# Attention products in column tiles of 32, and new orders at both ends of the shared feed-forward

## The chip, the cores and the metric

The kernel runs on one core of a Trainium2 chip. The metric is the device time of one execution in microseconds. TensorE is PE in the rows (its weight loads are PEld), VectorE is DVE, ScalarE is ACT, GpSimd is POOL, and SyncE is SP, which here only issues DMAs.

## The reference

Four sequences of 1024 tokens, 256 features. One layer: attention, then a mixture-of-experts feed-forward, each added to its input and normalised.

```python
Q, K, V = split_heads(x @ Wq.T), split_heads(x @ Wk.T), split_heads(x @ Wv.T)   # 16 heads of 16
Q, K = rope(Q), rope(K)
logits = where(causal, Q @ K.T * scale, -inf)
attn = softmax(logits) @ V
x = layernorm(x + merge(attn) @ Wo.T)
xf = layernorm(x) * ln_w + ln_b
e = argmax(xf @ router_w);  s = sigmoid(max(xf @ router_w))
routed = silu(s*xf @ gate_w[e]) * (s*xf @ up_w[e]) @ down_w[e]      # one of 8 experts a token
shared = silu(xf @ sh_gate) * (xf @ sh_up) @ sh_down
out = layernorm(x + x + routed + shared)
```

## The kernel before, in words

There are three stages. `project` (until about 113 us) makes queries, keys and values. `attend` (until about 539 us) works through 16 units, each one sequence and four heads. `feed` does the shared feed-forward on eight blocks of 512 tokens (540 to 731 us) and then 36 expert slots of 128 rows.

**Attention.** A unit has 12 steps. A step is one tile of 128 keys (`mt`) against one chunk of 512 queries (`c`); diagonal steps leave out queries before the keys, so a step is 512, 384, 256 or 128 queries wide. Per step PE makes the scores of four heads in two pairs (`score`, L1101), ACT takes the exponential (L1160), POOL zeroes what lies above the diagonal in diagonal steps (L1241), and PE multiplies by the values one step later (`times_v`, L1121). The values are stationary, 32 columns for each head, so the four heads stand in four column tiles of the array. ACT copies `out_ps` away after each chunk (L1168), and `times_v` of the next chunk's first step waits for that copy.

The exact row maximum is needed before the exponential. It is computed one or two units ahead, in 38 pieces of up to 512 columns per unit (`find_max`, L278), in a ring of three PSUM banks, and DVE reduces each piece (L320, or L315 with the mask added). A piece with 128 or 256 keys holds four or two heads; on its diagonal the mask is added by PE, with an identity as the weights (L282). `attend_plan` deals the pieces out to three slots in each step, in proportion to PE's work there: after each pair of scores and after `times_v`. In step 9 PE turns the finished maxima of the next unit (`turn_max`, L291, an fp32 transpose with 32 columns), ACT negates them (L300), POOL splits them in three, and SP sends them into `q_stack`.

`QUARTERS` cuts a product with 128 stationary columns in four matmuls with 32 columns each, which write partitions 0, 32, 64 and 96. `WHOLE` is one matmul. `Maxima.TILED` lists the slots in which scores and pieces with one head go in quarters: those of steps 4 to 6, 10 and 11 (with the last slot of steps 3 and 9) and slot 0. All else is whole, and so are all masks and the pieces with two or four heads. A unit has 48 score products, 48 maximum products and 16 mask products. Of these 8, 8 and 16 are 128 columns long, and 8, 8 and 0 are 256 long.

SP's queue holds, in order for each unit: the loads of the stacks of two units ahead, the stores of the heads, the sends of the maxima. In unit 12 `fill_tails` adds 16 transfers behind them.

**The shared feed-forward.** The front part of block i+1 (output projection, two layer norms, routing) lies between the products of block i. PE's order for a block is `gate` and `up` four times, `down` of tiles 0 and 1, `turn_xf` of the next block, `down` 2, `route`, `times_wo` of the block after, `down` 3, `count_ranks` (which waits for DVE's `choose`). `gate(i+1)` waits for `leave_xf_low`. `up(n)` waits for the product that DVE makes (`times_up`) of n-2, and `down(t)` for t of 2 and more waits for `add_shared(t-1)`. Block 0 runs `times_wo` of block 1 after its first `up`, and before that DVE turns the heads of block 1 at the start of the stage (L820). POOL takes the reciprocal roots (L966, L968), in one queue with its scatters (L1970, L1979). In the last block but one `make_tables` builds the expert tables, and then DVE copies the first expert's `up` weights (`copy_up(0)`, L1769) ahead of `times_up` 2 and 3 of the last block.

Of the kernel before, what the change touches and what calls it, by code (L numbers as in the profile page):

```python
# [29 lines left out]
P = 128  # L30
# [153 lines left out]

WHOLE = [(0, P)]
QUARTERS = [(a, a + SQUARE) for a in range(0, P, SQUARE)]


class Maxima:

    BANKS = 3


    TILED = {*range(3 * 3 + 2, 3 * 7), *range(3 * 9 + 2, 3 * 12), 0}

# [62 lines left out]

    def column_tiles(self, place):

        return QUARTERS if place in self.TILED else WHOLE

    def find_max(self, pe, u, which, place=None):

        if not u.exists():
            return
        nc = self.nc
        for n in which:
            h0, heads, t, chunk, keys = self.pieces[n]
            if n == 0:  # L270
                pe.wait_ge(self.loaded[u.slot], 16 * self.STACK_DMAS * (u.turn + 1))

            self.bank_free(pe, "piece", u.i, n)
            for k in range(heads):
                part = self.bank("piece", u.i, n)[:, k * keys:(k + 1) * keys]
                diagonal = chunk == t // BT and heads > 1
                for a, b in self.column_tiles(place) if heads == 1 else WHOLE:
                    last = nc.tensor.matmul(part[a:b], self.q_stack[:ROWS, u.slot, h0 + k, t * P + a:t * P + b],  # L278
                                            self.k_stack[:ROWS, u.slot, h0 + k, chunk * BLOCK:chunk * BLOCK + keys],
                                            start=True, stop=not diagonal)  # L280
                if diagonal:
                    last = nc.tensor.matmul(part[:, keys - P:], self.ident_bf[:], self.mask[:],  # L282
                                            start=False, stop=True)
            last.then_inc(self.piece_done, 1)
# [350 lines left out]
class Front:  # L635
# [253 lines left out]
    def norm_first(self, dve, i, batch, odd):  # L889
        nc = self.nc  # L890
        dve.wait_ge(self.rstd_made, 2 * i + 1)
        wait(dve, self.added, BT * (i - 1))
        for t in range(BT):
            last = nc.vector.tensor_scalar(self.x1[:, odd, t], self.res[:, odd, t], self.moments[:, t, 0:1],
                                           self.rstd[:, t:t + 1], ALU.subtract, ALU.mult)
        self.link(dve, i, last)
        self.take_moments(dve, i, self.x1[:, odd])

# [138 lines left out]
def attend(nc, io, keep, scratch):  # L1037
# [10 lines left out]
    with ExitStack() as ctx:  # L1048
# [43 lines left out]
        def _(pe):  # L1092
            def score(u, s, pair):
                c, mt, n0 = steps[s]
                if s == 0 and pair == 0:
                    pe.wait_ge(m.neg_loaded, 16 * PARTS * (u.i + 1))
                wait(pe, exp_done, 2 * (STEPS * u.i + s) + pair - 1)
                for k in range(2):
                    h = 2 * pair + k
                    for a, b in m.column_tiles(3 * s + pair):  # L1100
                        last = nc.tensor.matmul(scores_ps[a:b, pair, k, n0:],  # L1101
                                                k_stack[:ROWS_MAX, u.slot, h, mt * P + a:mt * P + b],
                                                q_stack[:ROWS_MAX, u.slot, h, c * BLOCK + n0:(c + 1) * BLOCK],
                                                start=True, stop=True)
                last.then_inc(scores_done, 1)
# [19 lines left out]
            def step(u):  # L1125
                for s in range(STEPS):
# [8 lines left out]
                    score(u, s, 0)  # L1135
                    m.find_max(pe, ahead, places[3 * s], 3 * s)
                    if s == 9:
                        m.turn_max(pe, u.ahead(1))
                    score(u, s, 1)
                    m.find_max(pe, ahead, places[3 * s + 1], 3 * s + 1)  # L1140
                    if (u.i, s) == OPEN["times_wo"]:
# [3 lines left out]
                    times_v(behind, (s - 1) % STEPS)  # L1145
                    m.find_max(pe, ahead, places[3 * s + 2], 3 * s + 2)

# [36 lines left out]
        def _(dve):  # L1184
            def step(u):
                for s in range(STEPS):
# [15 lines left out]
                    if (u.i, s) == OPEN["norm"]:  # L1202
                        f.norm_first(dve, 0, 0, 0)
                    if (u.i, s) == OPEN["scale"]:
                        f.scale_second(dve, 0, 0, 0)
                        f.shift_second(dve, 0, 0, 0)
# [4 lines left out]
                    if (u.i, s) == OPEN["route"]:  # L1211
                        f.choose(dve, 0, 0, 0)
                    for slot in range(3 * s, 3 * s + 3):
                        m.reduce(dve, u.ahead(1) if s < OWN_STEPS else u.ahead(2), places[slot])
# [63 lines left out]
def feed(nc, io, keep, scratch, out):  # L1278
# [16 lines left out]
    with ExitStack() as ctx:  # L1295
# [176 lines left out]
        def _(pe):  # L1472
# [112 lines left out]

            def block_step(i, odd, nxt, after):

# [3 lines left out]

                opening = isinstance(i, int) and i == 0
                for n in range(IC):
                    gate(i, n, odd)
                    up(i, n, odd)
                    if opening and n == 0:
                        front(f.times_wo)
                if opening:
# [17 lines left out]
                if nxt is None:  # L1616
                    expert_up(0)
                front(f.count_ranks)

            def step(batch):  # L1620
                last = isinstance(batch, int) and batch == BATCH - 1
                after = None if last else batch + 1
                block_step(2 * batch, 0, batch, after)
                block_step(2 * batch + 1, 1, after, after)

# [99 lines left out]
        def _(dve):  # L1725
# [145 lines left out]
            def block_step(i, odd, batch, nxt, after):  # L1871
# [8 lines left out]
                if nxt is not None:  # L1880
                    times_up(i, 0)
                front(f.norm_first)
                if behind:
                    f.find_place(dve, i, batch, odd)
                if nxt is not None:
                    times_up(i, 1)
                front(f.scale_second)
                times_up(i, 2)
                times_up(i, 3)
# [5 lines left out]
                if after is not None:  # L1895
                    f.turn_heads(dve, i + 2, after, odd)
                if nxt is not None:
                    f.leave_xf_low(dve, dve_stood, nc.vector.tensor_tensor, i + 1, nxt, 1 - odd)
                add_shared(i, 2, odd, batch)
                front(f.choose)  # L1900
# [10 lines left out]
            def step(batch):  # L1911
                last = isinstance(batch, int) and batch == BATCH - 1
                block_step(2 * batch, 0, batch, batch, None if last else batch + 1)
                if last:
                    make_tables()
                    dve.wait_ge(tables_made, 1)
                    dve.wait_ge(keep["weights_in"], 16 * 2 * EXPERTS)
                    copy_up(0)
                block_step(2 * batch + 1, 1, batch, *[None if last else batch + 1] * 2)
# [25 lines left out]
            f.make_score(dve, 0, 0, 0)  # L1945
            f.turn_heads(dve, 1, 0, 1)
            f.turn_out(dve, Unit.number(UNITS - 1), 1)
# [149 lines left out]
```

## Time and profile before

| | |
|---|---|
| median of three runs | 934.19 us (933.56 to 934.78) |
| the profiled execution: its own time, its span | 932.65 us, 930.9 us |
| PE busy | 904.8 us (97%), 8215 matmuls |
| PE weight loads | 570.3 us (61%) |
| DVE busy | 730.3 us (78%) |
| ACT busy | 469.6 us (50%) |
| POOL busy | 387.4 us (42%) |
| granted clock, mean | 0.995 of full |

All times inside the execution count from the start of the span. A matmul's row gives its start and its length, which includes about 0.18 us of passage through the array, so two neighbours overlap. The distance from start to start is what the engine pays. Where rows merge several matmuls ("x8"), the start is that of the first and the length runs to the end of the last.

### The profile page before, as it was taken

The page shows a single profiled execution, that of the slowest core. Times are in us where ns is not written, and L with a number is a line of the kernel's source. Part 1 is how long each engine was busy: PE and PEld are TensorE (multiplying, and loading weights), DVE is VectorE, ACT ScalarE, POOL GpSimd, SP SyncE. Part 2 cuts the span into 40 slices and gives each one's busy share as a digit, 9 for nine tenths or more (in the row PEclk, how much of TensorE's full clock was granted, in tenths as well). Part 3 has the DMA queues.
Part 4 walks back from the last instruction along what each step waited for, and adds up shares of the span by engine and source line. Part 5 has one row for each costly group of instructions (what it writes and reads, how often), then busy time and mean ns, then how long its engine had stood idle before and what let it go on. Part 6 is the DMA issues. An engine that isn't in the chain of part 4 may idle for free. (4 is left out here: it accounts for less than half of the span.)

```text
span 930.9 us, 23459 instructions
## 1 busy us (share of the span) xinstructions
PE 904.8 (97%) x8215; PEld 570.3 (61%) x8215; DVE 730.3 (78%) x1813; ACT 469.6 (50%) x655; POOL 387.4 (42%) x521
## 2 busy tenths in 40 slices
PE   9999899999999999999999889999999999999996
PEld 5556444444444444444434268888887999848996
DVE  5889899999999999999977657777777467575554
ACT  2454377777776777777656732222223232373321
POOL 8996232332233333323333421444446233333344
PEclk9999999999999999999999999999999999999999
DMA  8798344566665475856631186433345232223321
GB/s 315 187 252 241 55 64 64 59 82 87 105 82 93 58 108 62 126 76 82 142 42 13 13 244 210 144 90 93 92 144 177 78 95 75 68 65 86 82 71 41
DMA packets 174832, 99.25 MB, mean 107 GB/s; under 512 B 132480, under 2 KB 161408, under 8 KB 171520
## 3 DMA queue, kind: packets, MB, share of 16 engines
q1 hardware_dynamic: 161344, 71.85, 40.6%
q0 software_dynamic: 4800, 13.38, 3.9%
q10 hardware_dynamic: 8576, 12.58, 3.9%
q8 instruction: 64, 1.05, 0.5%
q14 instruction: 48, 0.39, 0.2%
HBM read 65.05 MB, written 32.31 MB: 105 GB/s over the span
## 5 line engine op out<-in xcount | busy, mean ns | idle before, releaser
L1160 ACT ACTIVATE probs<-scores_ps 128x1024 f32<-128x1024 f32 (+3 forms) x384 | 289.8, 810 | 96.4 <-PE scores_ps L1101 95.9
L320 DVE TENSOR_REDUCE maxima<-max_ps 128x1 f32<-128x512 f32 (+2 forms) x352 | 224.3, 680 | 28.6 <-PE max_ps L278 15.2
L278 PE MATMUL max_ps<-k_stack,q_stack 96*32 96x512 bf16 (+5 forms) x1731 | 224.5, 347 | 4.7 <-DMA q_stack<-q_parts 2.0
L1241 POOL TENSOR_SCALAR_AFFINE_SELECT probs<-probs 128x512 f32<-128x512 f32 x128 | 81.8, 639 | 261.7 <-ACT probs L1160 261.5
L1101 PE MATMUL scores_ps<-q_stack,k_stack 99*32 99x512 bf16 (+5 forms) x1824 | 186.3, 352 | 3.0 <-ACT probs L1160 1.4
L1121 PE MATMUL out_ps<-probs,v_ones 128*32 128x512 f32 (+3 forms) x1536 | 161.6, 493 | 3.9 <-POOL probs L1241 3.2
L315 DVE CUSTOM_DVE_ANT_0 masked_out<-max_ps,mask_wide 128x384 bf16<-128x384 f32 (+1 forms) x256 | 150.5, 617 | 7.1 <-PE max_ps L278 4.2
L278 PEld LDWEIGHTS max_ps<-k_stack,q_stack 96*32 96x32 bf16 (+1 forms) x1731 | 78.4, 95 | 107.1 <-DVE maxima L320 36.4
L1639 ACT ACTIVATE silu<-gate_ps 128x512 f32<-128x512 f32 x68 | 40.7, 598 | 184.1 <-PE gate_ps L1540 112.0
L1101 PEld LDWEIGHTS scores_ps<-q_stack,k_stack 99*32 99x32 bf16 (+1 forms) x1824 | 69.2, 97 | 92.7 <-ACT probs L1160 30.5
L2012 POOL DMA_INDIRECT out<-out_t,target_i x36 | 45.1, 1252 | 88.6 <-DVE out_t L1941 88.6
L1735 DVE TENSOR_TENSOR hidden_t<-silu,up_ps 128x512 f32<-128x512 f32 x36 | 24.8, 688 | 62.4 <-PE up_ps L1557 53.3
L1121 PEld LDWEIGHTS out_ps<-probs,v_ones 128*32 128x32 f32 x1536 | 36.2, 108 | 41.9 <-POOL probs L1241 17.5
L1540 PEld LDWEIGHTS gate_ps<-out_sb,heads_in 128*128 128x128 f32 x496 | 60.0, 192 | 2.3 <-issue 0.8
L1540 PE MATMUL gate_ps<-out_sb,heads_in 128*128 128x128 f32 x496 | 60.6, 275 | 0.0
L1557 PE MATMUL up_ps<-out_sb,res 128*128 128x128 f32 x496 | 60.5, 275 | 0.0
L1557 PEld LDWEIGHTS up_ps<-out_sb,res 128*128 128x128 f32 x496 | 57.9, 192 | 0.2
L464 PE MATMUL qk_ps<-x_t,w_qk 128*128 128x512 f32 x128 | 57.2, 600 | 0.0
L1503 PE MATMUL down_ps<-sh_down_sb,shared_t 128*128 128x256 f32 x184 | 45.6, 389 | 1.7 <-DVE total L1743 1.6
L282 PE MATMUL max_ps<-mask,ident_bf 128*128 128x128 bf16 x256 | 43.5, 221 | 0.0
L1476 PE MATMUL up_ps<-xf_split,sh_up_high 128*128 128x512 f32 x128 | 40.7, 399 | 1.8 <-DVE shared_t L1735 1.8
L1476 PE MATMUL gate_ps<-xf_split,sh_gate_high 128*128 128x512 f32 x128 | 41.0, 401 | 1.2 <-PEq L1048 1.2
(221 smaller groups left out, 1342.5 us busy)
## 6 DMA issues: line engine op xcount, KB each, us to landing
k_stack<-k_parts SPq DMA_DIRECT2D x96, 128.0 KB, 4.3
q_stack<-q_parts SPq DMA_DIRECT2D x96, 128.0 KB, 7.3
q_parts<-parts SPq DMA_DIRECT2D x32, 192.0 KB, 3.2
k_parts<-parts SPq DMA_DIRECT2D x32, 192.0 KB, 3.3
sums_in<-expert_sums SPq DMA_DIRECT2D x31, 136.0 KB, 2.1
heads_rows<-heads_out SPq DMA_DIRECT2D x128, 32.0 KB, 2.1
res<-in_x SPq DMA_DIRECT2D x8, 512.0 KB, 6.2
heads_in<-heads_rows SPq DMA_DIRECT2D x64, 64.0 KB, 4.1
```

The costliest lines, as they stand in the source:

```text
L278: last = nc.tensor.matmul(part[a:b], self.q_stack[:ROWS, u.slot, h0 + k, t * P + a:t * P + b], self.k_stack[:ROWS, u.slot, h0 + k, chunk * ...
L315: nc.vector.tensor_tensor_reduce(self.masked_out[:, n % 6, :keys], self.bank("piece", u.i, n)[:, :keys], self.mask_wide[:, BLOCK - keys:], ...
L320: nc.vector.tensor_reduce(self.maxima[:, u.slot, chunk, h0:h0 + heads, t], self.bank("piece", u.i, n)[:, :heads * keys].rearrange("p (h k) ...
L464: last = nc.tensor.matmul(qk_ps[:, k % 2, e], w_qk[:, which, c, e * P:(e + 1) * P], x_t[:, i, c], start=(c == 0), stop=(c == DC - 1))
L1101: last = nc.tensor.matmul(scores_ps[a:b, pair, k, n0:], k_stack[:ROWS_MAX, u.slot, h, mt * P + a:mt * P + b], q_stack[:ROWS_MAX, u.slot, h ...
L1121: last = nc.tensor.matmul(out_ps[32 * h:32 * h + 32, n0:], v_ones[:, u.slot, mt, h], probs[:, s % RING, h, n0:], start=(mt == 0), stop=las ...
L1160: nc.scalar.activation(probs[:, s % RING, 2 * pair:2 * pair + 2, n0:], scores_ps[:, pair, :, n0:], ACT.Exp).then_inc(exp_done, 1)
L1241: nc.gpsimd.affine_select(out=tile, in_=tile, compare_op=ALU.is_ge, fill=0.0, base=0, pattern=[[0, GROUP], [1, P]], channel_multiplier=-1) ...
L1476: last = nc.tensor.matmul(to_ps, weights[weight][:, c, n * P:(n + 1) * P].bitcast(F32R), f.xf_split[:, token, c].bitcast(F32R), start=(c = ...
L1503: last = nc.tensor.matmul(block_down(i, t), shared_t[:, c, t * P:(t + 1) * P], sh_down[:, c], start=(c == 0), stop=(c == IC - 1))
L1540: last = nc.tensor.matmul(gate_ps[:, j % 2, n * P:(n + 1) * P], gate_now[:, w % 2, c, n * P:(n + 1) * P], row_chunk(j, c), start=(c == 0), ...
L1557: last = nc.tensor.matmul(up_ps[:, j % 2, n * P:(n + 1) * P], up_now[:, w % 2, c, n * P:(n + 1) * P], row_chunk(j, c), start=(c == 0), sto ...
```

## The change

Every score, maximum and mask product of the units is cut in four column tiles. The maxima of the first unit and the early ones of the second, in the projection stage, stay whole. The rest changes orders in the feed-forward:

- `turn_heads` of block 1 goes from the start of `feed` to the last step 9 of attention on DVE, and in block 0 `times_wo` of block 1 goes ahead of the first `gate`.
- `norm_first` is split. In block 0 DVE makes `times_up(0, 1)` between the first norm and the second moments.
- DVE makes `add_shared(i, 2)` ahead of `leave_xf_low`, in every block.
- `count_ranks` of block 7 goes from the end of block 6 to behind the first `gate` of block 7.
- `times_up(7, 2)` goes ahead of `copy_up(0)`.

```diff
 class Maxima:
-    TILED = {*range(3 * 3 + 2, 3 * 7), *range(3 * 9 + 2, 3 * 12), 0}
...
-    def column_tiles(self, place):
-        return QUARTERS if place in self.TILED else WHOLE
-    def find_max(self, pe, u, which, place=None):
+    def find_max(self, pe, u, which, tiles=WHOLE):
...
-                for a, b in self.column_tiles(place) if heads == 1 else WHOLE:
+                for a, b in tiles:
                     last = nc.tensor.matmul(part[a:b], ...)
                 if diagonal:
-                    last = nc.tensor.matmul(part[:, keys - P:], self.ident_bf[:], self.mask[:],
-                                            start=False, stop=True)
+                    for a, b in tiles:
+                        last = nc.tensor.matmul(part[a:b, keys - P:], self.ident_bf[:, a:b], self.mask[:],
+                                                start=False, stop=True)
...
     def norm_first(self, dve, i, batch, odd):
...
         self.link(dve, i, last)
+
+    def second_moments(self, dve, i, batch, odd):
         self.take_moments(dve, i, self.x1[:, odd])
...
-                    for a, b in m.column_tiles(3 * s + pair):
+                    for a, b in QUARTERS:
...
-                    m.find_max(pe, ahead, places[3 * s], 3 * s)
+                    m.find_max(pe, ahead, places[3 * s], QUARTERS)
...
                     if (u.i, s) == OPEN["norm"]:
                         f.norm_first(dve, 0, 0, 0)
+                        f.second_moments(dve, 0, 0, 0)
...
                     if (u.i, s) == OPEN["route"]:
                         f.choose(dve, 0, 0, 0)
+                        f.turn_heads(dve, 1, 0, 1)
...
                 opening = isinstance(i, int) and i == 0
+                if opening:
+                    front(f.times_wo)
                 for n in range(IC):
                     gate(i, n, odd)
+                    if nxt is None and n == 0:
+                        f.count_ranks(pe, i, batch, odd)
                     up(i, n, odd)
-                    if opening and n == 0:
-                        front(f.times_wo)
...
-                front(f.count_ranks)
+                if after is not None:
+                    front(f.count_ranks)
...
                 front(f.norm_first)
+                opening = isinstance(i, int) and i == 0
+                if opening:
+                    times_up(i, 1)
+                front(f.second_moments)
                 if behind:
                     f.find_place(dve, i, batch, odd)
-                if nxt is not None:
+                if nxt is not None and not opening:
                     times_up(i, 1)
                 front(f.scale_second)
-                times_up(i, 2)
+                if nxt is not None:
+                    times_up(i, 2)
                 times_up(i, 3)
...
+                add_shared(i, 2, odd, batch)
                 if nxt is not None:
                     f.leave_xf_low(dve, dve_stood, nc.vector.tensor_tensor, i + 1, nxt, 1 - odd)
-                add_shared(i, 2, odd, batch)
...
                     dve.wait_ge(keep["weights_in"], 16 * 2 * EXPERTS)
+                    times_up(2 * batch + 1, 2)
                     copy_up(0)
...
             f.make_score(dve, 0, 0, 0)
-            f.turn_heads(dve, 1, 0, 1)
```

## Rows read from the trace of the kernel before

**Rows 1.** Stretch: its length; busy PE, PEld, DVE, ACT, POOL (instructions); clock, DMA share, GB/s.
```profile
231.04:257.62 26.58, 26.55 (x346) 12.22 (x343) 24.48 (x60) 19.11 (x27) 8.20 (x16) 1.00 0.56 92
257.62:284.20 26.58, 26.55 (x346) 12.11 (x343) 24.48 (x60) 19.21 (x27) 8.21 (x16) 1.00 0.63 91
```

**Rows 2.** PE in order of time, steps 7 and 8: start, length, engine, instruction.
```profile
255.49 0.40 PE L278 MATMUL max_ps<-k_stack,q_stack 96*32 96x512 bf16 x4
255.83 0.39 PE L1101 MATMUL scores_ps<-q_stack,k_stack 99*128 99x256 bf16 x2
...
256.50 0.38 PE L278 MATMUL max_ps<-k_stack,q_stack 96*128 96x512 bf16 x1
256.81 0.85 PE L1121 MATMUL out_ps<-probs,v_ones 128*32 128x384 f32 x8
```

**Rows 3.** PE: whole products of 256 and 128, the turn; then fp32 in four tiles.
```profile
259.79 0.27 PE L278 MATMUL max_ps<-k_stack,q_stack 96*128 96x256 bf16 x1
259.90 0.22 PE L282 MATMUL max_ps<-mask,ident_bf 128*128 128x128 bf16 x1
259.96 0.27 PE L291 MATMUL max_ps<-ident,maxima 128*32 128x128 f32 x1
...
530.64 0.62 PE L801 MATMUL max_ps<-xf_t,router_sb 128*32 128x128 f32 x16
531.20 1.04 PE L1101 MATMUL scores_ps<-q_stack,k_stack 99*128 99x512 bf16 x4
```

**Rows 4.** After the turn of the maxima in step 9: ACT, then PE.
```profile
260.44 3.80 ACT L1160 ACTIVATE probs<-scores_ps 128x1024 f32<-128x1024 f32 x4
262.40 0.61 PE L1101 MATMUL scores_ps<-q_stack,k_stack 99*32 99x512 bf16 x8
```

**Rows 5.** Around the copy of `out_ps`: PE, ACT, PE.
```profile
268.87 1.06 PE L1121 MATMUL out_ps<-probs,v_ones 128*32 128x512 f32 x8
270.00 0.59 ACT L1168 COPY out_sb<-out_ps 128x512 f32<-128x512 f32 x1 [0.45 <-PE out_ps L1121]
270.69 1.07 PE L1121 MATMUL out_ps<-probs,v_ones 128*32 128x512 f32 x8
```

**Rows 6.** DVE's reductions in one unit, two of those with idle time before them.
```profile
260.16 0.69 DVE L320 TENSOR_REDUCE maxima<-max_ps 128x2 f32<-128x512 f32 x1 [0.44 <-PE max_ps L282]
272.11 0.69 DVE L320 TENSOR_REDUCE maxima<-max_ps 128x1 f32<-128x512 f32 x1 [0.53 <-PE max_ps L278]
```

**Rows 7.** Unit 13's first piece for unit 15: SP's issue, PE.
```profile
458.34 2.76 SPq L234 DMA_DIRECT2D k_stack<-k_parts  x6
473.23 0.23 PE L278 MATMUL max_ps<-k_stack,q_stack 96*128 96x128 bf16 x1 [1.97 <-DMA q_stack<-q_parts]
```

**Rows 8.** The opening of the feed-forward: PE, DVE and POOL.
```profile
543.00 3.62 PE L779 MATMUL front_ps<-wo_t,heads_t 128*128 128x256 f32 x16
555.42 0.73 PE L1476 MATMUL up_ps<-xf_split,sh_up_high 128*128 128x512 f32 x2 [1.84 <-DVE shared_t L1735]
560.28 1.89 PE L1503 MATMUL hidden_ps<-sh_down_sb,shared_t 128*128 128x256 f32 x8
...
546.65 1.22 DVE L883 TENSOR_TENSOR res<-front_ps,res 128x1024 f32<-128x1024 f32 x1 [3.55 <-PE front_ps L779]
558.08 1.28 DVE L1735 TENSOR_TENSOR shared_t<-silu,up_ps 128x512 f32<-128x512 f32 x2
...
547.35 0.96 POOL L1970 DMA_INDIRECT expert_rows<-row,place_i  x1 [0.30 <-issue]
```

**Rows 9.** One stretch of the opening, columns as in rows 1.
```profile
555.00:560.00 5.00, 4.58 (x13) 3.67 (x14) 3.96 (x9) 0.60 (x1) 1.25 (x2) 0.66 1.13 349
```

**Rows 10.** The end of block 6 and the last block: PE and DVE.
```profile
708.24 1.99 PE L1503 MATMUL down_ps<-sh_down_sb,shared_t 128*128 128x256 f32 x8 [1.60 <-DVE total L1743]
706.62 1.23 DVE L837 TENSOR_TENSOR xf_split<-xf_t,xf_split 128x1024 fp32r<-128x1024 f32 x1 [2.71 <-ACT xf_split L831]
720.73 0.69 DVE L1769 COPY res<-up_sb 128x1024 f32 x1 [1.09 <-issue]
721.43 2.10 PE L1503 MATMUL down_ps<-sh_down_sb,shared_t 128*128 128x256 f32 x8
```

More of the change, by code:

```diff
@@ L1139, in step @@
                     score(u, s, 1)
-                    m.find_max(pe, ahead, places[3 * s + 1], 3 * s + 1)
+                    m.find_max(pe, ahead, places[3 * s + 1], QUARTERS)
                     if (u.i, s) == OPEN["times_wo"]:
@@ L1145, in step @@
                     times_v(behind, (s - 1) % STEPS)
-                    m.find_max(pe, ahead, places[3 * s + 2], 3 * s + 2)
+                    m.find_max(pe, ahead, places[3 * s + 2], QUARTERS)
             pe.wait_ge(m.k_ones, 1)
@@ L1584, in expert_down, with block_step @@
                 last.then_inc(down_done, 1)
-            def block_step(i, odd, nxt, after):
+            def block_step(i, odd, batch, nxt, after):
                 def front(part):
@@ L1622, in step @@
                 after = None if last else batch + 1
-                block_step(2 * batch, 0, batch, after)
-                block_step(2 * batch + 1, 1, after, after)
+                block_step(2 * batch, 0, batch, batch, after)
+                block_step(2 * batch + 1, 1, batch, after, after)
             pe.wait_ge(f.split_step, f.SPLITS_MADE)
```

## The prediction

> **What bounds the kernel now.** I read the page's busy times first, then the slices, then stretches of one unit, then PE's timeline in such a stretch, and beside it those of DVE, ACT, POOL and SP. The page has PE at 97% and DVE at 78% over the span, but attention and feed-forward differ. In attention one unit takes 26.58 us, and the next has the same length and the same counts: PE 26.55 busy, DVE 24.48, ACT 19.1, POOL 8.2 [rows 1]. PE sets the pace and DVE stands 2.1 us behind it. What the busy time hides is seen only from start to start. A product of 512 bf16 columns takes 512/2.4 GHz = 0.213 us, whole or in four tiles that run side by side. But from the last tiled maximum (255.49) to the first whole score (255.83) it is 0.34 us, so 0.12 to 0.13 us are lost, and from a whole maximum (256.50) to the tiled value product (256.81) it is 0.31, so 0.10 are lost [rows 2]. Nothing waits there; the loss comes with the change between whole and tiled. The value products are always tiled, so each of the steps 7, 8, 9, 0, 1, 2 and 3, where scores and maxima are whole, costs a change to and a change back: seven of each in a unit, the timeline shows them all at nearly these prices.
>
> In the shared feed-forward PE is busy without a gap in blocks 1 to 5; idle time stands only in block 0 (1.84 us before `up` 3) and at the end of block 6 (1.60 us) [rows 8, 10].
>
> **Attention, the gain.** Seven pairs of changes at 0.12 + 0.09 (the low ends, since a few ns lie between any two products) are 1.48 us a unit. Three things take from it.
> - `turn_max` is an fp32 transpose of 32 columns amid whole products, and it starts (259.96) 0.06 us after the mask product before it (259.90), which is that product's own 128 columns: no loss [rows 3]. It is a whole-array operation in effect and is not changed. With tiled neighbours it now costs a pair of its own: -0.21.
> - The last value product of a unit starts at 268.87; its result is copied from 270.00, and the first value product of the new unit follows at 270.69 [rows 5]. These 1.82 us are product, copy and passage, and don't shrink. PE's own work in them (0.86, then two maxima of 0.213 and four short scores of 0.056) is 1.51 us. The pair of changes in there is won and waited away: -0.21.
> - DVE. It has idle time for the gain: 2.1 us a unit, in five waits for maxima of which 0.44 and 0.53 are the longest, and they stand just where the changes of steps 8 to 2 delay a piece [rows 6]. Between them, from step 2 to step 8, it works 13 us on end, with only three banks to let PE run ahead. At a period of 25.6 it would be 96% busy. I take 0.13 off for waits that it now causes.
>
> That makes 1.48 - 0.21 - 0.21 - 0.13 = 0.93 us a unit. A cross-check is the ACT path of step 9: `turn_max` at 259.96, exponentials from 260.44, the second pair of scores of step 10 at 262.40 [rows 3, 4]. It starts from `turn_max`, which has five changes before it (0.12, 0.09, 0.12, 0.09, 0.12) and one new one, so this point comes 0.45 earlier, and the second half of the unit gains as much again.
>
> **Attention, the cost.** 32 products a unit have 128 columns and will be four matmuls with four weight loads in place of one each. No bf16 product of this length is tiled before. Whole, the next one starts 0.06 later (259.90, 259.96). The nearest tiled row is the router's: 16 fp32 matmuls of 128 columns from 530.64 to 531.20, which is 0.44 after taking off a change of 0.12, or 0.110 for four [rows 3]. fp32 at 256 cycles needs 0.107 for that, so no cost per matmul is seen above the columns. From below, bf16 costs its columns, 0.056, and nothing is added (a gain is excluded, the columns are the same). From above it costs as much as that row, 0.110: 32 x 0.054 = +1.7 us a unit. I take the lower end, since the row is explained by its columns, and keep the upper one as a rival. The 256-column products (0.107 of columns) lie at the row's pace already. The additional weight loads run beside the matmuls.
>
> The Trainium skill says otherwise: by "TensorE: Matmul & The Clock Gate", section "Wait — 56ns, not 53.3ns?", matmuls never start less than about 25 ns apart, however short. By that page four tiles would take about 0.100 us in place of 0.056, an estimate of +1.4 us a unit, which eats the whole gain of attention. The router's row has 27 ns a matmul and neither bears that out nor refutes it.
>
> **How many units.** Units 0 to 14 have maxima of a later unit to compute. Two parts of one are off. Unit 14 has none after step 7. And in unit 13 the first piece of unit 15 waits 1.97 us for its stacks, whose load SP issues only at 458.34, behind the 16 transfers of `fill_tails`; it lands at 473.2 [rows 7]. SP's queue there starts from the sending of the maxima in step 9 of unit 12, and from there to the landing it takes the same time whatever PE does. What PE gains in between makes that wait longer: one unit's gain is lost. 13.8 units are left: 13.8 x 0.93 = 12.8 us. In unit 15 there are no maxima, and the path runs from scores over exponential and mask to the value products; a change back mostly falls into a wait, a change to whole stands on the path in a few steps: 0.4 us.
>
> **The opening of the feed-forward.** `times_wo` of block 1 starts at 540.13 (the first `gate` before) in place of 543.00. `add_heads` on DVE so starts at about 543.7 in place of 546.65 [rows 8]. POOL, however, is in its four scatters of block 0 until 548.31 (the last starts at 547.35 and takes 0.96), so the reciprocal root comes at 549.7 (0.3 + 1.05 us) in place of 551.4. First norm until 551.15, then at once the `times_up(0, 1)` until 551.8, before PE needs it for `up` 3 (553.4). The 1.84 us stall goes. What is late next is DVE again: second moments (1.93) until 553.7, root until 555.3, `scale_second` (1.7) until 557.0, `times_up` 2 and 3 until 558.2. Before, these two ran from 558.08 to 559.3. So `down` of tile 0 ends at about 558.75, and tile 1 starts there in place of 560.28: 1.5 us won, of 1.84. PE stands idle about 1.8 us inside `down` 0, as long as before. Before, the granted clock fell to its lower level, 1.2 GHz, shortly after the stall: its mean of 0.66 over 5 us makes that 3.4 us [rows 9]. If it does again, at a worse place, up to 1.5 us go. I take 0.9. `turn_heads` (1.25 us) moves to a DVE that is idle for 4 us there and costs nothing; without that cover it would delay block 0's `find_place` by 1.25 us, which has 1.5 us to spare.
>
> **The end.** At 708.24 PE has waited 1.60 us for `add_shared(6, 2)`, which stood behind `leave_xf_low` (706.62, 1.15 long), which waited for ACT [rows 10]. With the add first, `down` 3 starts at about 706.6. `leave_xf_low` stays where it is, so `choose` ends only 0.3 earlier (709.6); `count_ranks`, behind `gate` 0, comes just after it, at 709.75. That is 1.7 us on PE. Given back: `up` 3 waits 0.1 for tables and `times_up(7, 1)` on DVE, which gain only 0.4. `times_up(7, 2)` fits in the 1.09 us in which DVE waits for a register load ahead of `copy_up(0)` (720.73), but `times_up(7, 3)` comes behind the copy, at 721.5. So `down` 0 of block 7, at 721.43 before, starts at 719.8 and waits 0.5 for it. 1.2 to 1.3 us stay, since rows for the first slot are turned at about 724.8, before PE asks. In blocks 1 to 5 the add ahead of `leave_xf_low` fills DVE's own wait: 0.
>
> **Sum.** 12.8 + 0.4 + 0.9 + 1.3 = 15.4 us. Span 930.9 - 15.4 = 915.5; the profiled execution, 1.75 above its span, 917.2; the median of the runs lies 1.5 above that one: 918.8.
>
> **Rivals.**
> - *DVE and the waits take half* (0.18). With 96% on DVE and three banks, each unit gains 0.45. For it: 13 us of DVE without a gap, and that reductions wait for nothing but PE. Against: the idle places lie where the gain arises. 13.8 x 0.45 + 2.6 = 8.8, so 925.4.
> - *Short tiles cost their issue, and it is slower* (0.09). The place is the stretch of steps 8 and 9 and of 0 and 1, where 32 short products lie close. If four matmuls take more than 0.056 + 1.08/32 = 0.090 us, attention loses. At the router's 0.110 a unit is 1.7 - 0.95 = 0.75 longer (DVE no longer waited for), 15 units +11 us, less 2.6 at the ends: 942.8. At an average over a unit it means 544 matmuls in place of 335, 46 ns each, and the shortest distance over a long stretch (512-column tiles, 0.213 for four) is 53 ns, so a supply limit is not excluded. Against: that pace is the columns' own.
> - *The skill's floor, as a rival* (0.05), worked out from rows: at 0.100 for four a unit costs 32 x 0.044 = 1.4, less 0.95: +0.45, 15 units +6.8, less 2.6 is 938.4. The page named above gives the figure of 25 ns.
> - *More comes back* (0.10): neighbours of the value products gain also in their first pass, DVE causes no wait, and `turn_max` costs no change: 1.27 a unit, 13.8 x 1.27 + 3.5 = 21.0, so 913.2.
> - The forecast (0.58), 915 to 922.5.
>
> **From these** the range is 911 to 930; the remaining 2 in 10 are the slow cases and a part of DVE's; of these two groups 0.02 each end within or beyond the bound on the other side. A difference of 0.2% (1.9 us) is what can be told from no change. Faster 0.84, same 0.04, slower 0.12.
>
> **What would show it.** In the profile after: periods of about 25.65 us with DVE at 24.5 busy; value products that start 0.22 after a 512-wide maximum in step 8; short products in fours at 0.056 to 0.060; `turn_max` with 0.1 lost on both sides; the wait in unit 13 near 2.9 us; `down` 1 of block 0 1.5 us closer to the start of the stage; no wait ahead of `down` 3 of block 6. The forecast is wrong if fours of 128 columns start 0.09 or more apart, or if the period is above 26.2.

## The result and the profile after

The changed kernel takes 940.57 us (median of 7 runs, 936.79 to 944.94) beside 933.87 for the kernel before: a ratio of 1.0081, 95% interval [1.0054, 1.0107]. It is 0.8% slower. The forecast was 918.8, so both the sign and the size were wrong.

The pace itself came as forecast. First come two periods of the changed kernel, one quiet and one not (columns as in [rows 1]):

```profile
235.74:261.51 25.77, 25.55 (x549) 13.11 (x549) 24.47 (x60) 19.29 (x28) 8.20 (x16) 1.00 0.63 95
315.17:346.79 31.62, 27.39 (x549) 15.10 (x549) 24.80 (x60) 19.44 (x28) 9.29 (x18) 0.95 0.65 95
```

The quiet period is 25.77 us, against 26.58 before [rows 1]. The other has the same 549 matmuls (545 of the unit's own and a few that cross the window's edges), and takes 5.85 us more. Short products in four tiles, PE in order of time:

```profile
313.07 0.24 PE L273 MATMUL max_ps<-k_stack,q_stack 96*32 96x128 bf16 x4
313.12 0.24 PE L278 MATMUL max_ps<-mask,ident_bf 128*32 128x128 bf16 x4
313.18 0.24 PE L273 MATMUL max_ps<-k_stack,q_stack 96*32 96x128 bf16 x4
```

Fours start 0.055 to 0.06 us apart, where 128 columns at 2.4 GHz are 0.053: next to nothing comes on top. What is new stands in the list of PE's waits over 100 to 520 us (line, releaser, us in total, times, longest), where before there was next to no `issue`:

```profile
PE scores_ps L1099 <- issue: 8.6, 6, 2.7
PE max_ps L273 <- issue: 7.7, 4, 4.1
PE max_ps L273 <- DMA q_stack<-q_parts: 3.8, 1, 3.8
PE out_ps L1119 <- issue: 0.2, 1, 0.2
```

For 16.5 us PE stands still although nothing that the profile knows of holds it. One such place, in order of time, and the two windows from it on (columns as in [rows 1]):

```profile
330.72 0.39 PE L273 MATMUL max_ps<-k_stack,q_stack 96*32 96x512 bf16 x3
335.17 0.38 PE L273 MATMUL max_ps<-k_stack,q_stack 96*32 96x512 bf16 x4 [4.06 <-issue]
```
```profile
331.00:336.00 5.00, 0.94 (x16) 0.60 (x16) 1.14 (x3) 1.29 (x2) 0.25 (x1) 0.99 1.05 182
336.00:341.00 5.00, 5.00 (x64) 2.76 (x59) 3.32 (x11) 2.63 (x3) 0.63 (x1) 0.67 0.62 90
```

The gap falls within one maximum product, between two of its tiles, so no semaphore is meant. The DMA engines are full (share 1.05). The granted clock then falls to its lower level, 1.2 GHz, for 3.4 us (mean 0.67 over 5 us). The trace has five such stretches between 200 and 600 us, where before had two. A third view, the page's busy line (matmuls behind the x) and its row of the instruction queue, of the changed kernel and then of the kernel before:

```profile
PE 895.9 (95%) x11302; PEld 599.5 (64%) x11302; DVE 733.4 (78%) x1813; ACT 472.2 (50%) x655; POOL 386.5 (41%) x521
...
q8 instruction: 88, 1.44, 0.7%
```
```profile
q8 instruction: 64, 1.05, 0.5%
```

88 packets of 16 KB fit 2 x 11302 matmuls and weight loads at 256 instructions a packet; the 64 before fit 2 x 8215. So q8 brings PE's instructions. Counting PE's records from the start, its sequencer's included, each of the ten gaps over 0.3 us comes at the same place: record 193 or 194 of a group of 256. (From here on a group, or block, is the 256 records from one such place to the next.) The packets of q8 from the changed kernel's trace, in us, beside the time at which PE reaches those records:

```
previous group begins   packet begins, ends   next group begins   idle of PE
294.70                  294.85   295.77       300.71              none
300.71                  304.18   305.84       307.22              0.33
325.31                  331.84   333.55       335.17              4.06
385.53                  392.30   393.43       394.71              2.35
```

A packet is triggered when PE enters the group before. Half of them start within 1.2 us of that entry and have landed within 2.3. Beside a stack load a packet starts up to 6.8 us late. In the ten gaps PE goes on 1.3 to 1.8 us after it has landed. A group lasts 4 to 7.4 us in the changed kernel where neither a gap nor the lower clock is in it, and 8 to 11 before. That was the theory for the experiments: PE uses up its instructions faster than the fetch, held up by the packets of the stack loads, brings the next 16 KB.

The Trainium skill, "Runtime: NRT & Kernel Launch", section "Instruction fetch mechanics", says that instructions come in 16 KiB blocks of 256 by the sequencer's own DMA queue, one block ahead. The packets agree (88 of 16 KB, one per 256 records). It calls the crossing "mostly hidden"; here ten crossings cost 16.4 of the 16.5 us.

The stretch used below is the time from the first to the last of the sixteen copies of the turned maxima (`negate` on ACT): 402.93 us before, 416.33 after. From the last copy to the end of the span it is 428.1 and 427.1.

### The profile page after: what moved, and what is told of

Read it like the earlier page. It is cut to its first block and busy times, and to the rows that moved or that the text cites. A ratio compares the mean times of both kernels' runs of the same rounds, so it can differ in the third digit from the quotient of the medians.

```text
span 942.6 us, 29633 instructions
## 1 busy us (share of the span) xinstructions
PE 895.9 (95%) x11302; PEld 599.5 (64%) x11302; DVE 733.4 (78%) x1813; ACT 472.2 (50%) x655; POOL 386.5 (41%) x521
## 5 line engine op out<-in xcount | busy, mean ns | idle before, releaser
L273 PE MATMUL max_ps<-k_stack,q_stack 96*32 96x512 bf16 (+5 forms) x2874 | 243.6, 331 | 14.7 <-issue 7.7
L1099 PE MATMUL scores_ps<-q_stack,k_stack 99*32 99x512 bf16 (+3 forms) x3072 | 198.3, 330 | 12.0 <-issue 8.6
L1119 PE MATMUL out_ps<-probs,v_ones 128*32 128x512 f32 (+3 forms) x1536 | 165.6, 494 | 6.3 <-POOL probs L1241 3.7
L273 PEld LDWEIGHTS max_ps<-k_stack,q_stack 96*32 96x32 bf16 (+1 forms) x2874 | 91.1, 96 | 101.0 <-DVE maxima L316 32.8
L1099 PEld LDWEIGHTS scores_ps<-q_stack,k_stack 99*32 99x32 bf16 x3072 | 85.4, 98 | 95.3 <-issue 42.6
L1119 PEld LDWEIGHTS out_ps<-probs,v_ones 128*32 128x32 f32 x1536 | 43.8, 110 | 29.3 <-POOL probs L1241 8.9
L278 PE MATMUL max_ps<-mask,ident_bf 128*32 128x128 bf16 (+1 forms) x952 | 46.0, 222 | 0.0
L460 PEld LDWEIGHTS qk_ps<-x_t,w_qk 128*128 128x128 f32 x128 | 24.4, 192 | 27.3 <-issue 27.0
```

The lines of the kernel that those rows point to most:

```text
L460: last = nc.tensor.matmul(qk_ps[:, k % 2, e], w_qk[:, which, c, e * P:(e + 1) * P], x_t[:, i, c], start=(c == 0), stop=(c == DC - 1))
L1099: last = nc.tensor.matmul(scores_ps[a:b, pair, k, n0:], k_stack[:ROWS_MAX, u.slot, h, mt * P + a:mt * P + b], q_stack[:ROWS_MAX, u.slot, h ...
L1119: last = nc.tensor.matmul(out_ps[32 * h:32 * h + 32, n0:], v_ones[:, u.slot, mt, h], probs[:, s % RING, h, n0:], start=(mt == 0), stop=las ...
```

## The experiments

**Which part loses.** The first kernel is the change without its attention part, the second its attention part alone.

> The attention as it was (TILED and whole mask products), only the new orders of the opening and the end of the feed-forward. Theory (instruction supply in the attention makes the loss): the ends bring what the changed kernel's own trace shows behind the last turn of maxima, about 1 us, so 931.3 to 933.3, a ratio of 0.997 to 1.000. Forecast on record: 2.2 us gained, 931.7. Rival (the ends lose what is missing): slower than before, 936 to 940.

Measured: 931.68, ratio 0.9978 [0.9962, 0.9994].

> The ends as they were, every attention product in four tiles. Theory: the whole loss is here; the unit's own pace falls to 25.7 us, but PE stands idle at 16 KB steps of its instructions; 940 to 944, ratio 1.007 to 1.011. Rival (the ends lose): 920 to 925.

Measured: 943.30, ratio 1.0109 [1.0086, 1.0132]. The loss is all in the attention; the ends gain 1.6 us.

**Lighter loads.** For units 3 to 15:

```
-  stack[e*DK:(e+1)*DK, u.slot]    <- all heads of the part
+  stack[e*DK:(e+1)*DK, u.slot, 0] <- head 0 of the part
```

> The changed kernel, but the stack loads of units 3 to 15 move one head in four (as many transfers, a quarter of the bytes; the other heads keep the data of an older unit), so the DMA engines are no longer full for 12 to 14 us of each unit. Theory (the fetch of the next 16 KB of PE's instructions waits behind the packets of these loads): PE's idle time with no releaser in the attention falls from 16 us to under 2, the periods are all 25.7 to 26, time 919 to 924. Rival A (tiles need more instructions than PE's sequencer can take, whatever the DMA does): the idle time stays, 938 to 943. Rival B (only part of it is the fetch; the lowered clocks come from elsewhere): 926 to 933.

Measured: 915.96, ratio 0.9814 [0.9792, 0.9836]. The longest of PE's waits from 100 to 520 us, and one period:

```profile
PE out_ps L1124 <- POOL probs L1246: 3.7, 9, 0.7
```
```profile
203.50:229.26 25.76, 25.54 (x549) 13.16 (x548) 24.46 (x60) 19.28 (x28) 8.23 (x16) 1.00 0.21 40
```

There is no wait on `issue` left, every fetch lands within 3.35 us of its trigger, the stretch is 387.27, and all periods but the first are 25.67 to 25.84. There is no stretch at half clock before the feed-forward. The same instructions run, so they alone were not too many. It came out 3 us below the expected range; the wait for the last stack (3.8 us) went too. The other corner of the square:

> The kernel before, with the stack loads of units 3 to 15 cut to one head in four. Theory (with 335 pairs per unit the fetch of instructions is in time even beside full loads): only the wait for the last stack (2.0 us), the 0.3 us at 334 us and the 0.4 us of one longer period go: 930 to 932.5. Rival (light loads speed the units themselves, whatever the tiles): under 927.

Measured: 928.86, ratio 0.9959 [0.9942, 0.9976], stretch 399.07, periods still 26.58; 1 us below the expected range. So light loads bring 3 us without the new tiles, and 25 with them.

**The same bytes, spread.** SP issues one transfer per pair of heads:

```
-  wait(sp, scores_done, 2 * STEPS * (u.i - 2))
-  m.load(sp, u, range(m.STACK_DMAS))
+  for n in range(m.STACK_DMAS):
+      wait(sp, scores_done, 2 * STEPS * (u.i - 2) + n)
+      m.load(sp, u, [n])
```

> The changed kernel with all bytes of the stack loads, but SP issues the twelve transfers one at a time, one for each pair of heads whose scores are done (about 1.07 us apart; one transfer gives each DMA engine one packet of 8 KB of 1.04 us), so that no backlog builds up in front of the instruction fetch. Theory (the wait behind the backlog is what makes the fetch late, not the bandwidth): fetches of PE's instructions start within about 2 us of their block instead of up to 6.5, idle time under 4 us, 920 to 927. Rival A (the fetch needs free bandwidth, the pace of the issues changes nothing): 938 to 943. Rival B (the loads land later than the first maximum products of the unit after next need them): a wait for q_stack in step 8 of every unit, over 945.

Measured: 924.57, ratio 0.9909 [0.9885, 0.9933]. No `issue` wait; nine fetches in ten land within 3.0 us of their trigger (5.3 in the changed kernel). The bytes are the same, so it is the backlog ahead of the fetch, not the bandwidth. Two other waits are left, for transfers queued on SP:

```profile
PE scores_ps L1100 <- DMA q_stack<-neg_parts: 3.4, 2, 2.1
...
PE max_ps L273 <- DMA q_stack<-q_parts: 2.1, 1, 2.1
```

> The kernel before with the paced stack loads alone. Theory: before has 335 pairs per unit, 16 KB last 8 to 11 us, and the late fetch cost it 0.3 us in one place only, so the pace brings nothing: 931 to 935, ratio 0.998 to 1.002 (up to 3 us more if the heads' and the maxima's transfers behind it on SP are late, as they were in two units with the pace and the tiles). Rival (the pace is a gain of its own, the tiles had no part in the loss): 916 to 926.

Measured: 932.59, ratio 0.9994 [0.9983, 1.0006]. Without the new tiles the pace is worth nothing, as expected.

**Count or tiles?** In the kernel before, each score product is cut in two by columns, and each maximum product of one head in the same way (not shown):

```
+  half = (n0 + BLOCK) // 2
+  for x, y in ((n0, half), (half, BLOCK)):
       for a, b in m.column_tiles(3 * s + pair):
-          matmul(scores_ps[a:b, pair, k, n0:], ...)
+          matmul(scores_ps[a:b, pair, k, x:y], ...)
```

> The kernel before with its tiles where they were, but each score product and each maximum product of one head in two halves of its columns: about as many pairs per unit (some 570) as the changed kernel, with not one more product in tiles and the same columns in all. Theory (it is the count of instructions, not the tiles): PE stands idle without releaser at 16 KB steps of its instructions during the loads, as in the changed kernel, 10 to 20 us in all; 942 to 955. Rival (it is the tiles): 933 to 936.

Measured: 970.16, ratio 1.0396 [1.0374, 1.0418]. The rival is out: with no additional tile, PE waits for 26.0 us on `issue`:

```profile
PE max_ps L280 <- issue: 16.2, 7, 4.4
PE scores_ps L1106 <- issue: 9.8, 5, 2.2
```

The size is 15 us above the expected range: more idle time than I allowed, 24 us at half clock up to 510 us, and a period that is longer even where nothing waits (26.9 to 27.1, where it was 26.58), which is a price of the cuts themselves.

**Fewer instructions.** One mask product serves all heads of a bank:

```
-  for each head k: matmul(part[a:b, keys - P:], ident_bf[:, a:b], mask, start=False)
+  once: matmul(full[a:b, :, keys - P:], ident_bf[:, a:b], mask.to_broadcast([P, heads, P]), start=False)
```

> The changed kernel with one mask product for all heads of a bank (a 3D pattern of 4 x 128 or 2 x 128 columns) in place of one for each head: 40 of some 544 pairs of weight load and matmul less per unit (7%), the same columns, so PE's work in us stays. Theory (the rate at which instructions are used up, against a fetch that is late in each load): blocks last longer, idle time without releaser falls from 16.5 us to 9 to 14, time 934 to 939. Rival (the count of instructions doesn't matter): 939 to 942.

Measured: 924.74, ratio 0.9918 [0.9903, 0.9933]; `issue` waits 3.1 us in all. That was far better than expected, and my reading of it as a count effect did not survive the next run. A unit has 1015 of PE's records here, 3.96 groups of 256 (the expectations count from windows, which gives a few too many or too few), so the crossing falls at nearly the same place in each unit. 32 short products at the start, which leave 128 more records in the trace, shift it by half a group:

> The changed kernel with one mask product per bank, and 32 short products of 16 columns more at the very start, which move every later step from one 16 KB block of PE's instructions to the next by half a block. One mask product per bank makes a unit 1018 instructions long, 3.98 blocks, so the steps fell at nearly the same place of each unit. Theory A (the loss fell from 16.5 us of idle time to 3 because 40 pairs fewer slow the consumption): unchanged by the shift, first to last turn of the maxima 395 to 397 us. Theory B (it fell because the step came to lie where the load does no harm): the stretch changes by more than 2 us either way, up to 410 us where the step falls behind a dense place during the load, or down to 387. The start itself costs 1 to 4 us more.

Measured: 954.22, ratio 1.0212 [1.017, 1.0255]. Stretch 421.24, where it was 395.85 without the shift and 410 was the most I expected; the start is 5.4 us longer (the clock rose to full only at 13.5 us, in the others at 4 to 7). PE's waits:

```profile
PE max_ps L273 <- issue: 7.3, 4, 3.1
PE scores_ps L1103 <- issue: 7.2, 4, 3.0
PE max_ps L273 <- DMA q_stack<-q_parts: 5.0, 1, 5.0
...
PE out_ps L1123 <- issue: 1.3, 2, 1.0
```

So half a group of instructions is worth 25 us: the fewer masks had gained by their place (theory B). The two traces show the place. In both, every gap has a packet that was triggered during a stack load. With the shift, 12 of the 21 triggers that fall in a load come 3.3 to 6 us after its first packet; they land 4.4 to 8.6 us later, and all nine gaps follow from them. Without it one of 27 comes there, and it gives the worst gap, 0.9 us; the others come earlier or later, and none of them costs more than 0.6 us.

**Is it the place for the others too?**

> The changed kernel with the shift by half a block. A unit is 1090 instructions long, 4.26 blocks, so the steps walk through all places of a unit within four units whatever the shift. Theory: the stretch stays within 8 us of the changed kernel's 416.33, total 938 to 954 with the 5.4 us of the start. Rival (the changed kernel had a specially bad place): the stretch under 405.

Measured: 942.47, ratio 1.0095 [1.0064, 1.0126], stretch 415.47. A unit of 4.28 groups (1095 records) walks through all places, and the shift changes nothing. The total came out in its range although the start cost 1.8 us and not 5.4.

> The kernel before with the shift by half a block. Theory (16 KB last 8 to 11 us here, longer than the latest fetch takes): stretch 402 to 405, as 402.93 without it, total 937 to 940. Rival (before was at a lucky place): stretch over 407.

Measured: 934.95, ratio 1.0022 [1.0012, 1.0033], stretch 402.62. The time lies below its range, since the start cost 1.2 us here, not 5.4. The kernel before has the slack, but only just: with the shift, fetches take up to 10.0 us from their trigger, three `issue` waits come (1.1 us in all), and four periods are 0.4 to 1.1 us longer than 26.6, where one was. The wait for the last stack, 0.8 us in place of 2.0, and no lower clock behind it make up for them.

**A version that beats both.** Pace, and on SP the heads' loads behind the sending of the maxima and the tails two units later:

```
-  if u.i in (GROUPS + 4, GROUPS + 6): ... f.load(sp, odd, 0, odd)   # ahead of send_neg
   m.send_neg(sp, u.ahead(1))
-  if u.i == GROUPS + 8: f.fill_tails(sp)
+  if u.i in (GROUPS + 4, GROUPS + 6): ... f.load(sp, odd, 0, odd)
+  if u.i == UNITS - 2: f.fill_tails(sp)
```

> The changed kernel with the paced stack loads, and on SP the loads of the heads for the opening moved behind the transfer of the maxima of the same unit, and the filling of the tails moved from unit 12 to unit 14, where no stack is loaded any more. Theory: of what the paced kernel still lost, the waits for neg_parts (2.1 and 1.3 us) and for the last stack (2.1) go: 917 to 921. Rival (the transfers moved hit the next unit's stack load or the opening as hard): 923 to 927.

Measured: 916.67, ratio 0.9827 [0.9811, 0.9844], stretch 389.89. The waits for the maxima's transfers are gone; of the moved transfers one new wait for a stack came (1.8 us), for one that went.

> One mask product per bank, with the paced stack loads and the moved transfers of SP. Theory: the pace has taken the late fetches away already, so fewer masks bring nothing more: 915 to 918.5, as with the pace and the moved transfers alone. Rival (some late fetches are left, or fewer products help PE itself): under 915.

Measured: 915.44, ratio 0.9807 [0.9782, 0.9833], 1.9% faster than before. Stretch 388.49; two periods and the longest of PE's waits:

```profile
204.62:230.38 25.76, 25.52 (x509) 12.78 (x509) 24.46 (x60) 19.30 (x27) 8.19 (x16) 1.00 0.49 86
230.38:256.14 25.76, 25.51 (x509) 12.67 (x509) 24.46 (x60) 19.30 (x28) 8.19 (x16) 1.00 0.53 95
```
```profile
PE out_ps L1122 <- POOL probs L1244: 5.7, 21, 0.7
```

> One mask product per bank, paced loads and moved transfers, with the shift by half a block. Theory (the pace keeps every fetch in time, so the place of the step is of no account): first to last turn 388.5 to 390 us as without the shift (388.49), the total 5.4 us longer for the products at the start, 919.5 to 922. Rival (the place of the step matters without a backlog too): stretch over 392.

Measured: 920.69, ratio 0.9892 [0.9857, 0.9926], stretch 390.25, just outside the 388.5 to 390 expected. Its two longer periods (27.81, 27.08) hold waits for stacks; of gaps at a group's edge there is one, of 0.3 us. The shift that cost 25 us of the stretch without the pace costs 1.8 with it. That the total fell in its range is luck: the start took 1.5 us more and not 5.4, and the profiled executions are 3.4 us apart where the medians are 5.2.

> The same as the fewer masks with the pace and the moved transfers, but the opening of the shared feed-forward in the old order (on PE and on DVE), the new end kept. Theory (the new opening brings the second normalisation 1.06 us forward, and PE's longer wait before it is followed by a stretch at half clock that takes 1.6 back, which the old order had not in the kernel with the tiles alone): 0.3 to 0.8 faster, 915 to 917.5. Rival (the half clock comes with either order): 1 us slower, 917 to 919.

Measured: 916.92, ratio 0.9828 [0.9802, 0.9855]. In both profiles the last copy to the end takes 426.9 to 427.0 us, and both have the stretch at half clock (from 541.2 and 543.3). Neither order of the opening is shown better here.

## Why the prediction was wrong, step by step

**The step that failed** is one clause in the cost of the attention part, "the additional weight loads run beside the matmuls", and with it the sum over a unit as PE's pace alone. Beside the matmuls they do run: 549 pairs in the quiet period take 25.77 us. But they are also instructions to be fetched. A unit went from 341 pairs to 545 (windows as in [rows 1] count 346 and 549, the forecast 335 and 544), so 256 instructions last 4 to 7 us in place of 8 to 11, and both rows of [rows 1] with their DMA share of 0.56 and 0.63 hide a load with the engines full for 10 to 12 us. During such a load a fetch takes up to 8.2 us in the changed kernel. This is shown by cutting the loads (-25 us, and only -3 without the new tiles), spreading them (-16 and nothing) and raising the count without tiles (+37, of which 26 are `issue` waits).

The bill against the forecast in the profiled execution: 944.36 less 917.2 is 27.2 us. The `issue` waits are 16.5. Four stretches at half clock lie in the attention where before had one; each lasts 3.4 us and costs half of that, so three more are an estimated 5.1. All four begin within 1.6 us of a gap of PE (three `issue` waits and the wait for the last stack), and with light loads the attention has none. The stack wait of unit 13 is 3.8 in place of 2.9: 0.9. Without waits the stretch would be 387.3, as with light loads, and not 385.5 (402.93 - 12.8, less the wait of 2.9 and one half-clock stretch): 1.8. Behind the last copy 1.6 of the forecast gain are missing, and the first copy comes 0.7 earlier. That is 25.2; 2.0 us are not traced.

**Seven pairs of changes won, less three deductions, 0.93 us a unit**: right but for a little. The quiet periods give 26.58 - 25.76 = 0.82. DVE stayed out of it (24.47 busy), and that rival fell.

**Unit 15, 0.4 us**: did not come. From the last copy to the first `gate` of the feed-forward it is 37.32 us before and 37.34 with the tiles alone.

**Short tiles cost their columns**: right, 0.055 to 0.06 for four. Both rivals that priced a short four at 0.100 or 0.110 fell, although their times, 938.4 and 942.8, lie beside the measured one: a right number from a wrong mechanism, which is luck. The text did say that "a supply limit is not excluded", yet looked for it in an average over a unit, 46 ns a pair. The average is no limit: with light loads it runs free.

The floor of the Trainium skill, about 25 ns between matmul starts ("TensorE: Matmul & The Clock Gate", section "Wait — 56ns, not 53.3ns?"), does not hold across four column tiles: in the rows above a new four starts every 0.058 us, 14.5 ns for each matmul. The section speaks of matmuls back to back and not of tiles; carrying the figure over to them was the forecast's own step.

**Unit 13**: the wait grew from 1.97 [rows 7] to 3.8, more than the 2.9 forecast. That it grew by the gain of the units is not shown: the same attention with the old ends waits 2.0 us there, and with the shift 4.2. The gaps shift PE against SP's transfers, so each kernel meets them elsewhere.

**The opening**: mechanism right, size taken back by the clock. The rows of the changed kernel are POOL's last scatter and the root behind it, then PE's second half of `down` 1:

```profile
560.04 0.96 POOL L1978 DMA_INDIRECT expert_rows<-row,place_i  x1 [0.30 <-DVE moments L871]
561.04 0.25 POOL L964 TENSOR_SCALAR var_eps<-moments 128x4 f32<-128x4 f32 x1
```
```profile
570.42 1.46 PE L1503 MATMUL down_ps<-sh_down_sb,shared_t 128*128 128x256 f32 x4 [1.71 <-DVE shared_t L1738]
571.68 3.46 PE L1503 MATMUL hidden_ps<-sh_down_sb,shared_t 128*128 128x256 f32 x8
```

The first root waits for POOL's scatters, as worked out. `hidden_ps` takes 3.46 us, where it takes 1.89 [rows 8] at full clock; 1.6 us go. The kernel with fewer masks had no lower clock there:

```profile
550.60 1.30 PE L1505 MATMUL down_ps<-sh_down_sb,shared_t 128*128 128x256 f32 x4 [1.89 <-DVE shared_t L1740]
551.74 1.89 PE L1505 MATMUL hidden_ps<-sh_down_sb,shared_t 128*128 128x256 f32 x8
```

Its block 1 starts 66.47 us behind the last copy. With the old opening, also at full clock (tiles alone), that is 67.57: 1.1 us won, where 0.9 was forecast. At half clock it is 68.16, against 67.87 before, whose own low stretch [rows 9] fell elsewhere. The forecast did name this ("at a worse place, up to 1.5 us go").

**The end**: right. From the start of block 1 to the first `expert_gate` it is 156.14 us before and 154.86 after, 1.28 won of a forecast 1.3.

**The chances.** 0.12 for slower was too little. The price of the loads that "run beside the matmuls" was bounded by what an instruction takes in the array, never by what it takes to bring it.

## What to carry to other kernels

Count the instructions of the engine that sets the pace, and where they are densest compare how long 256 of them last with the latest fetch beside the largest burst of DMA (here 8 to 10 us). If they are shorter, spread the burst first: one transfer per pair of heads, a packet per engine at a time, gave 16 us back and cost nothing by itself, although transfers queued behind it on SP came late in two units (3.4 us). And where the fetch is late and a loop body lies near a whole number of blocks, believe no gain or loss of 1 to 3% from a small edit before the same kernel has run with its instructions shifted by half a block. Of four kernels shifted here, the one that had both moved by 25 us; the other three moved by 2 us at most.

## What the runs showed that I had not expected

- A PE wait on `issue` in the middle of a product's four tiles is a missing instruction block: in all kernels with such gaps they stand at record 193 or 194 of 256. Without the pace, every packet that came too late had been triggered during a stack load; outside the loads all packets land within 3.6 us of their trigger (from 110 to 470 us). PE goes on 1.2 to 2.0 us after the packet has landed.
- The packet of 16 KB itself takes 0.9 to 1.9 us; the rest of up to 8.6 us from its trigger (10.0 in a kernel with the old tiles) is waiting beside 8 KB packets of about 1 us.
- 32 products of 16 columns at the very start delay the first copy by 1.2 to 1.8 us in three kernels and by 5.4 in the fourth, where the clock rose later. Why only there stays open, as does why a packet waits behind several of the load's packets and not behind one.
